# A graph network block on one core: masks, softmax denominators and weight splits of the attention stage rearranged between the engines

## What is computed

```python
HW = h @ W
row, col = (edge_index[0], edge_index[1])
s = HW @ a[:OUT_F, 0]
t = HW @ a[OUT_F:, 0]
e = leaky_relu(s[row] + t[col])
m = segment_max(e, row)
ex = exp(e - m[row])
den = segment_sum(ex, row)
agg = segment_sum((ex / den[row])[:, None] * h[col], row)
out = silu(agg) @ base_w.T + einsum('nip,oip->no', b_splines(agg), spline_w)
```

## Time and profile before

| | us |
|---|---|
| median of 3 runs | 684.33 (682.5 to 684.81) |
| the profiled execution | 683.7 |
| its span | 681.9 |
| TensorE busy | 604.3 (89%) |
| VectorE busy | 477.9 (70%) |
| ScalarE busy | 371.5 (54%) |
| GpSimd busy | 23.3 (3%) |

### The profile page before, as it was taken

The page is one execution under the profiler, slowest core; times in us unless marked ns, Lnnn a source line. Parts: engine busy times, 40 slices in busy tenths (PEclk is TensorE's granted clock), DMA queues, the critical chain, the costliest instruction groups (busy, mean ns, idle before and its releaser), DMA issues.

```text
span 681.9 us, 8727 instructions
## 1 busy us (share of the span) xinstructions
PE 604.3 (89%) x3437; PEld 428.2 (63%) x3437; DVE 477.9 (70%) x739; ACT 371.5 (54%) x486; POOL 23.3 (3%) x30
## 2 busy tenths in 40 slices
PE   3766655999968999999999999869999999999994
PEld 2535643555534455555555555448999899988994
DVE  7989698999785999997369865784344434542354
ACT  1798597545779998987198620328331422332111
POOL 2000000000000000000000000202300020000000
PEclk9798686999979899999999999979999999999998
DMA  8553400000040000000001000090100000001202
GB/s 278 192 186 126 195 1 0 1 1 1 0 151 0 2 1 0 1 1 1 1 1 62 1 0 1 23 369 15 62 1 1 0 1 1 1 0 56 94 38 113
DMA packets 11417, 33.73 MB, mean 49 GB/s; under 512 B 718, under 2 KB 1038, under 8 KB 11120
## 3 DMA queue, kind: packets, MB, share of 16 engines
q1 hardware_dynamic: 11376, 33.17, 13.8%
HBM read 24.78 MB, written 8.40 MB: 49 GB/s over the span
## 4 chain that ended last, share of the span: by engine, by line
PE 67%; DVE 18%; ACT 8%; issue 4%; DVEq 1%; ACTq 1%; DMA 0%; SPq 0%
PE bank L1482 32%; PE bank L1557 20%; PE bank L1526 12%; DVE AL L994 2%; DVE OR L847 2%; DVE OM L850 2%; DVE EX L987 1%; DVE EX L999 1%; DVE SCR L958 1%; ACT CT L599 1%; PE bank L1328 1%; ACT JSQ L532 1%; ACT WKh L606 1%; DVE RDN L1029 1%; DVE hL L1004 1%
## 5 line engine op out<-in xcount | busy, mean ns | idle before, releaser
L1482 PE MATMUL bank<-BHL,WKh 128*128 128x418 f16 x1152 | 207.1, 342 | 4.2 <-DVE BHL L1083 4.2
L1482 PEld LDWEIGHTS bank<-BHL,WKh 128*128 128x128 f16 x1152 | 112.0, 97 | 99.3 <-DVE BHL L1083 4.6
L1557 PE MATMUL bank<-CF,YL 128*128 128x418 f32 x360 | 127.5, 354 | 0.0
L1557 PE MATMUL bank<-CF,YH 128*128 128x418 f32 x360 | 126.6, 352 | 0.0
L1277 DVE TENSOR_TENSOR Z<-bank,dvb 128x418 f32<-128x418 f32 x36 | 21.3, 593 | 69.1 <-PE bank L1557 69.1
L1557 PEld LDWEIGHTS bank<-CF,YL 128*128 128x128 f32 x360 | 67.6, 188 | 1.8
L1557 PEld LDWEIGHTS bank<-CF,YH 128*128 128x128 f32 x360 | 67.7, 188 | 1.0
L784 ACT ACTIVATE bnc<-bnm,tiny 128x1 f32<-128x1 f32 x12 | 3.5, 294 | 104.9 <-DVE bnm L1283 104.9
L1335 PE MATMUL bank<-OM,OR 128*128 128x160 f16 x320 | 32.3, 268 | 19.7 <-DVE OM L850 13.7
L1228 DVE SCALAR_TENSOR_TENSOR YL<-bank,dvc,YH 128x512 fp32r<-128x512 f32 x30 | 21.9, 748 | 38.5 <-ACT YH L765 38.5
L1526 PE MATMUL bank<-GWH,XH 128*128 128x512 f32 x120 | 48.1, 401 | 0.0
(11 more groups left out here) (202 smaller groups left out, 1010.6 us busy)
## 6 DMA issues: line engine op xcount, KB each, us to landing
WKf<-in_wk SPq DMA_DIRECT2D x9, 1024.0 KB, 5.4
c_scratch<-C SPq DMA_DIRECT2D x1, 3200.0 KB, 10.9
GWf<-in_gwT SPq DMA_DIRECT2D x3, 1024.0 KB, 5.4
C<-c_scratch SPq DMA_DIRECT2D x1, 2880.0 KB, 10.4
XT<-in_xT SPq DMA_DIRECT2D x1, 2500.0 KB, 8.8
x_scratch<-XT SPq DMA_DIRECT2D x1, 2500.0 KB, 16.1
XR<-x_scratch SPq DMA_DIRECT2D x1, 2500.0 KB, 8.9
outT<-Z SPq DMA_DIRECT2D x4, 625.0 KB, 3.1
```

The source lines that it names most:

```text
L1482: ins = mm(bank[:, 4 * (g % 2) + o, 0:G], lhs, rhs, start=(u == 0 and q == 0 and i == 0), stop=(u == UNITS - 1 and q == PAIR - 1 and i == 2))
L1557: ins = mm(bank[:, YB + u % YB, 0:G], Y[:, j, o * P:(o + 1) * P], CF[:, j, g * G:(g + 1) * G], start=(j == 0 and i == 0), stop=(j == NT - ...
```

## The change

The words of the change: masks on GpSimd, and softmax denominators from products with the weights stationary and one moving column, inverted as columns. The diff does the following.

1. GpSimd writes the ten masks (six buffers) and the ten low feature parts: six masks, then, after the columns of t, four feature parts, then masks and parts in turn.
2. VectorE's projections read the rows of W times a from PSUM; `WAB` is gone. All ten projections of s follow those of t. A bound on |t| is taken from the sum of squares of the row of a (ScalarE, L543's place: a square and a root); it is added to the ten columns of t before they are spread, so that the row maximum is taken from PSUM directly. The maximum over the row and `U` are gone.
3. TensorE: one transposed row, the spread of t, the degrees, then the other nine rows, on two banks in turn. The spread of the inverse root degrees comes after the first set of columns and after all transposes.
4. ScalarE: squares of blocks 3 and 4 behind the first transposed row; blocks 5 to 8 at items 1, 3, 5 and 7 of the loop, behind the high copy. The table load for the exponential is before the first rows.
5. Denominators: for each group 80 products with 128 x 128 weights stationary and one column of ones moving (four parts of the 418 columns, ten tiles, high and low), after unit 2; VectorE clamps and inverts a 128 x 4 tile; TensorE spreads it after unit 3 (four float32 products); VectorE copies the row to `RDN`. Unit 0's 20 products are gone.
6. The ten half-blocks are split inside the loop, at items 16 to 25: high part behind the high copy on ScalarE, low part behind `attention_f32` on VectorE.

```diff
@@ gpsimd
+            pool.wait_ge(counts_final, 1)
+            pool.wait_ge(sub_copied, GROUPS)
+            def mask(s):
+                if s >= MASKS:
+                    pool.wait_ge(masked, s - MASKS + 1)
+                nc.gpsimd.tensor_scalar(MSK[:, s % MASKS, :], C16[:, s, :], 1.0, None, ALU.min).then_inc(mask_set, 1)
+            def feature_rest(t):
+                pool.wait_ge(h_high, t + 1)
+                nc.gpsimd.tensor_tensor(hL[:, t, :], hx[:, t, :], hH[:, t, :], ALU.subtract).then_inc(h_low, 1)
+            for s in range(MASKS):
+                mask(s)
+            pool.wait_ge(t_cols, 1)
+            for t in range(4):
+                feature_rest(t)
+            for s in range(MASKS, NT):
+                mask(s)
+                feature_rest(s - 2)
...
@@ scalar
+            transposed(0)
+            sum_squares(3, JSQ)
+            sum_squares(4, JSQ)
             act.wait_ge(degs_done, 1)
...
-            for t in range(5, NT):
+            for t in range(1, NT):
                 transposed(t)
...
+            nc.scalar.activation(mv[:, 0, 0:1], tiny[:, 0:1], ACT.Exp)
+            attention_rows(0)
             act.wait_ge(dv_spread, 1)
...
             attention_rows(1)
...
             exponentials(0)
+            attention_rows(2)
             for n in range(NG * NT):
                 g, j = divmod(n, NT)
                 if n + 1 < NG * NT:
                     exponentials(n + 1)
                 act.wait_ge(att_f32, n + 1)
                 nc.scalar.copy(CT[:, j, g * G:(g + 1) * G], EX[:, n % 3, :]).then_inc(att_high, 1)
+                if n in LATE_SQUARES:
+                    sum_squares(5 + LATE_SQUARES.index(n), JSQ3)
+                if FIRST_HALF <= n < FIRST_HALF + LATE:
+                    weights_high(n - FIRST_HALF)
...
             silu_of(0, 0)
-            weights_high(0)
-            weights_high(1)
             silu_high(0, 0)
...
@@ vector
             for n in range(NG * NT):
                 if n + 1 < NG * NT:
                     attention_sum(n + 1)
-                if n < NT:
-                    feature_rest(n)
...
                 if n >= 1:
                     attention_low(n - 1)
                 attention_f32(n)
                 if n == 9:
+                    dve.wait_ge(squares, KB)
+                    V.tensor_reduce(wsc[:, 0:1], wss[:, :], AX, ALU.add).then_inc(sumsq_set, 1)
+                if n == 13:
                     weight_scale()
-                if n == 12:
+                if n == 14:
                     denominators(0)
+                if n == 15:
+                    denominator_row(0)
                     aggregated(0, 0)
...
+                if FIRST_HALF <= n < FIRST_HALF + LATE:
+                    weights_low(n - FIRST_HALF)
+                if n == 22:
+                    denominators(1)
                 if n == 23:
+                    denominator_row(1)
                     aggregated(1, 0)
...
             silu_low(0, 0)
             silu_low(0, 1)
             denominators(2)
             silu_low(1, 0)
+            silu_low(1, 1)
+            denominator_row(2)
             for c in range(DC):
                 aggregated(2, c)
...
@@ tensor
+            def weight_sums(g):
+                for i, c0 in enumerate(PARTS):
+                    out = bank[:, att_bank(g, 0), DEN_AT + i:DEN_AT + i + 1]
+                    for j in range(NT):
+                        for low in range(2):
+                            m = low_weights(g)[:, j, c0:c0 + P] if low else CT[:, j, g * G + c0:g * G + c0 + P]
+                            ins = mm(out, m, ones16[:, 0:1], start=(j == 0 and low == 0), stop=(j == NT - 1 and low == 1))
...
             for g in range(NG):
                 if g == 1:
-                    pe.wait_ge(pq_set, NG)
+                    pe.wait_ge(wscale_set, 1)
...
-                for k in range(DC + 1):
+                for k in range(1, DC + 1):
                     for j in range(NT - LASTS, NT):
                         pe.wait_ge(att_low, g * NT + j + 1)
                         attend(g, k, j)
...
+                    if k == 2:
+                        if g >= 1:
+                            pe.wait_ge(agg_out, DC * g)
+                        weight_sums(g)
+                    if k == 3:
+                        sums_spread(g)
...
-            pe.wait_ge(den_out, NG)
-            pe.wait_ge(agg_out, 2 * DC + 1)
+            pe.wait_ge(rden_set, NG)
+            pe.wait_ge(agg_out, 2 * DC)
             pe.wait_ge(wk_low, HALVES)
             silu_units(0)
```

More of the change, by code:

```diff
@@ L67 @@
 EARLY_SQUARES = (6, 8, 11)
+LATE_SQUARES = (1, 3, 5, 7)
 LASTS = 3
+MASKS = 6
+PARTS = (0, P, 2 * P, G - P)
+DEN_AT = 480
+BOUND = 1.02
+FIRST_HALF = 16
 SETS = ((0, 4), (4, 7), (7, 10))
@@ L189, in build @@
         RDN = small("RDN", [G])
+        RDC = small("RDC", [NG, len(PARTS)])
         dvb_at = z5[0]
@@ L462, in _ @@
             nc.gpsimd.tensor_copy(AB[:, :, :], wide(acol[:, :], P)).then_inc(ab_set, 1)
+            pool.wait_ge(counts_final, 1)
[15 more added lines that the diff above has]
+                feature_rest(s - 2)
+            for t in range(NT - 2, NT):
+                feature_rest(t)
             pool.wait_ge(agg_unit, (DC + 1) * NG)
@@ L542, in _ @@
                     act.wait_ge(wa_spread, 1)
-                    nc.scalar.copy(WAB[:, :, :], bank[:, 6:8, :]).then_inc(wa_set, 1)
+                    nc.scalar.activation(JST[:, 0, :], bank[:, 7, :], ACT.Square, accum_out=tb[:, 0:1])
+                    act.drain()
+                    nc.scalar.activation(tb[:, 1:2], tb[:, 0:1], ACT.Sqrt, bias=tiny[:, 0:1], scale=BOUND * D
+                                         ).then_inc(t_bound, 1)
                 if 13 <= n < 13 + NT // 2:
@@ L554, in transposed @@
                     act.wait_ge(tposed, 2 * t + b + 1)
-                    nc.scalar.copy(CT[:, t, 5 * b * P:5 * (b + 1) * P], bank16[:, 4 + 2 * (t % 2) + b, 0:5 * P]
+                    nc.scalar.copy(CT[:, t, 5 * b * P:5 * (b + 1) * P], bank16[:, 4 + b, 0:5 * P]
                                    ).then_inc(tposed_out, 1)
-            for t in range(5):
-                transposed(t)
+            transposed(0)
+            sum_squares(3, JSQ)
+            sum_squares(4, JSQ)
             act.wait_ge(degs_done, 1)
             nc.scalar.activation(dvc[:, :], bank[:, 3, 0:NT], ACT.Sqrt, bias=1.0).then_inc(degs_out, 1)
[L562 to L565, removed]
-            for t in range(5, NT):
+            act.wait_ge(squares, 5)
+            for t in range(1, NT):
                 transposed(t)
@@ L976, in _ @@
                 columns(i)
+                if i == 0:
+                    dve.wait_ge(degs_out, 1)
+                    V.reciprocal(dvc[:, :], dvc[:, :]).then_inc(dvc_set, 1)
             dve.wait_ge(c16_out, 16)
@@ L1383, in _, with degrees @@
             pe.wait_ge(consts_set, 2)
-            pe.wait_ge(wa_set, 1)
-            def degrees(t0, t1):
-                for t in range(t0, t1):
+            def degrees():
+                for t in range(NT):
                     for s in range(NT):
@@ L1460, in _ @@
                         attend(g, k, j)
+                    if g == 0 and k == 1:
+                        pe.wait_ge(sumsq_set, 1)
+                        mm(bank[:, 2, 0:1], ones[:, :], wsc[:, 0:1], start=True, stop=True).then_inc(sumsq_done, 1)
+                    if k == 2:
[4 more added lines that the diff above has]
+                        sums_spread(g)
             def means(g):
```

194 lines of the change are left out of this document (74 added, 120 removed).

## The result

| us | before | after |
|---|---|---|
| median of 4 runs each | 684.08 (682.5 to 684.81) | 700.14 (699.76 to 701.12) |
| the profiled execution | 683.7 | 701.12 |
| its span | 681.9 | 699.0 |
| GpSimd busy | 23.3 | 68.7 |

The changed kernel is slower: ratio 1.024, interval 1.0219 to 1.0261, 16 us. The forecast of 687.5 had the sign but not the size, and the time lies outside its range, 682.6 to 694.0. The loop came out as forecast, the tail nearly; the start lost 6.1 us where I had it gain 8.2.

The account below looks back on a forecast made before the run. It took the wait chain up to TensorE's long stretch to bound the kernel: start -8.2, loop +23.5, tail -12.1, sum +3.2 us, so 687.5 us on the median of 684.33; range 682.6 to 694.0.

Parts of the forecast that it names:

- The loop: From the attention's first high copy to the end of the last low weights: 89.8 us for 66.3, +23.5 us.
- the tail: From the last low weights' end to TensorE's long stretch at full clock: 33.1 us for 45.2, -12.1 us.
- the start: Up to the attention's first high copy: at 106.1 us instead of 114.33, -8.2 us.
- dear rival: Start, GpSimd masks at 2.9 us each: last mask at 106.9, first high copy at 113.4, +7.3, 694.8 us; chance 0.12.
- lock rival: Start: VectorE's small operations wait for the GpSimd operation in progress, up to +4.9, 692.4 us; chance 0.16.
- T: Time when the attention's last low weights end on VectorE: forecast 195.9 us, before the change 180.62.
- the long stretch: TensorE working alone without a gap after the attention: forecast to start at full clock at T + 33.1, 229.0 us.
- The spline chain: Tail: work that readies the first spline unit, forecast done at T + 31.2, before TensorE ends its SiLU products.
- "not slower" rival: Start and tail: fetch stall hidden at full clock (-2.4), gap costs no clock (-1.9); both give 683.2 us; chance 0.30.

Follow-up runs that it names:

- run 2: Kernel before the change plus twelve extra GpSimd operations (minimum, product, copy, sum of two tensors) at a quiet place, drains between; ran once, 684.94 us.
- run 1: Changed kernel with the ten masks back on VectorE, only the low feature parts left on GpSimd; 686.97 us, ratio 1.004.
- run 4: Kernel before the change with only the ten low feature parts moved to GpSimd; 690.68 us, ratio 1.0098.
- Run 5: Changed kernel with VectorE's low part of each weight half-block one item later in its queue; 685.2 us, ratio 1.0018.
- Run 7: Changed kernel with the squares of blocks 5 to 8 moved ahead of the loop; 696.2 us, ratio 1.0175.
- run 8: Changed kernel with masks back on VectorE and low weight parts one item later, together; 671.96 us, ratio 0.9826.
- run 9: Kernel of run 8 with the squares of blocks 5 and 6 also ahead of the loop; 670.63 us, ratio to the kernel before 0.9811.
- run 11: Kernel of run 8 with the third attention rows copied behind the first high copy; 671.41 us, ratio to the kernel before 0.9821.
- run 12: Kernel of run 9 with the third attention rows copied behind the first high copy; 667.75 us, ratio to the kernel before 0.9763.
- run 10: Kernel of run 8 with each group's 80 one-column weight sums issued twice; 677.27 us, ratio to the kernel before 0.9901.
- run 6: Changed kernel with the expert-weight half-blocks split behind the loop again, woven into the SiLU items; 690.82 us, ratio 1.0099.

## Why the prediction was wrong

**The start, the step that failed: "I take the copy's rate, since a mask has one input: 1.3 us for 1280 columns".** A mask took 3.42. No row of the trace before has that operation on GpSimd. The upper end that I kept, 2.9 us from the two-input operation, rested on the same idea, that inputs set the price, and was no upper end; run 2 shows that a scalar costs more than a second tensor. The range ended at 694.0, below even the 694.8 of my own dear rival. With the right price the working of the dear rival holds. It had the last mask at 106.9; ten times 0.52 us more, and a first mask at 70.48 instead of 69.5 (less 0.4 for parts of 1.14), give 112.7, and the trace has 112.46. From there the rival needs 6.5 us to the first high copy, the trace took 8.0: 120.44.

**The missing 1.4 us are the lock rival's.** The third set of columns took from 114.12 to 116.14, 2.0 us for 0.64, while GpSimd formed the last feature parts. At other places a small operation waited up to 2.87 us (74.05), since a mask is a long instruction to wait for; those fell in time that the masks cost anyway. The two rivals, given 0.16 and 0.12 as if one excluded the other, came together. The masks were dearer than I had priced them; the lock held a single operation longer (2.87 us for 0.17, where I had allowed 1.3 more) but cost only 1.4 on the path, in the third set, where the rival had none. 13.2 us of the 16 went with the masks (run 1). With masks on VectorE the start is 109.1, 5.2 us better than before and not 8.2: there VectorE's masks, maxima and columns end at 104.8, and TensorE is not late. No run has GpSimd masks at the price I took, so the 106.1 itself was not tried.

What I had right in the start: ScalarE's last transposed copy ended at 94.3 (forecast 95.0), the degrees ran 100 products in 2.64 us without the stop of 2.99 us (that it was a fetch is shown by no run), and maxima that read t from PSUM stayed at 1.48 beside GpSimd, which run 4 sets against 2.44 for those that read U from SBUF. The Trainium skill (SBUF — State Buffer, "Who interferes with whom") states that a VectorE operation with at most one SBUF input, outside its two-port modes, doesn't contend with GpSimd; here the traces agree.

**The loop was right.** 89.2 us for 89.8; copies of the weight items 4.52 us apart for 4.54; VectorE idle 1.66 before the low part, released by ScalarE. Run 5 shows that the order within the item is the cause: one item later, with no work removed, gave 14.9 us. Run 7 puts 4.6 us on the four squares, forecast as 4 x (4.64 - 3.41) = 4.9.

**The tail was right to 2 us.** T + 31.3 for T + 33.1. The gap ahead of the 96 SiLU products (3.42 us) cost no clock: they took 17.17 us, 0.179 each, where I had added 2.8 us. This isn't a rule: behind the same gap, 3.42 or 3.43 us, these 96 took 18.84, 18.85, 18.84, 18.72, 18.84, 18.78 and 18.85 us in runs 1, 5, 7, 8, 9, 11 and 12. That it cost nothing here is luck, but a small one: where the clock fell, in run 1, the long stretch began at T + 31.8. The term that I had too large is the 2.8 us, which measured 1.6 or nothing. The spline chain was ready at T + 31.3, for T + 31.2; the SiLU products were done before it, so 0.96 us of the old idle time of 4.15 stayed, where the forecast had none.

**The sum.** 120.44 + 89.2 + 31.3 = 240.9 against the forecast 106.1 + 89.8 + 33.1 = 229.0: +14.3, -0.6, -1.8. The "not slower" rival fell with the masks too, though both its conditions came true: the degrees had no stop and the gap cost no clock.

## What to carry to other kernels

Before work is moved to GpSimd, time that very operation there: 1280 columns with a scalar took 3.42 us and a copy rate said 1.3. Count the neighbours too, since a VectorE operation with two SBUF inputs waits nearly to the end of the GpSimd instruction in progress, however small it is (100.53 to 102.96 for three columns, beside a mask that ends at 103.38). And where one engine prepares what another finishes, let the second take it one item later: the same work in the same loop cost 1.75 us an item less.

## What I had not expected

- GpSimd's operation with one tensor and a scalar costs 2.51 ns a column, that with two tensors 1.67, the copy 0.83, float16 and float32 alike.
- VectorE's mask, one float16 input and a scalar, also slows beside GpSimd: 2.88 us for two in place of 0.83, and 1.32 for 0.49 (runs 1 and 4). I had thought of the lock for operations with two inputs alone. The Trainium skill (SBUF — State Buffer, "Who interferes with whom") does name tensor_scalar among those that can take the shared ports; the traces agree.
- An idle gap of 3.42 us ahead of TensorE's 96 products cost some 1.6 us of clock in seven kernels and nothing in the changed one; behind 1.41 us (run 10) or none (run 6) they took 17.17 and 17.16.
- The 80 one-column products of a group, each with its own weights, took 1.98 us, 0.025 each, at full clock.
